# q and k parts as eight products with one store each, and attention's first loads and tiles moved into the last batch of the first layer

## What is computed

```python
# layer 0: a feed-forward block whose weights are picked per batch by an index
h = gelu(x @ Wi[e] + bi[e]);  o = h @ Wo[e] + bo[e]         # 256 -> 1024 -> 256
x = layernorm(o + x) * g[e] + be[e]
# layer 1: a transformer block
x = layernorm(x) * (1 + scale) + shift                      # from a time-step embedding
q, k, v = heads(x @ Wq + bq), heads(x @ Wk + bk), heads(x @ Wv + bv)   # 16 heads of 16
scores = q / 4 @ k.T + attention_bias                       # bias: 8 x 16 x 512 x 512 f32, 134 MB
scores = where(src_mask, -inf, scores)
x = x + (softmax(scores) @ v) @ Wo + bo
x = x + gelu2((layernorm(x) * g2 + beta2) @ W1 + b1) @ W2 + b2
```

## Time and profile before

| | us |
|---|---|
| median of 3 runs (lowest, highest) | 1185.88 (1183.18, 1190.21) |
| the profiled execution, its own time | 1181.05 |
| its span in the trace | 1179.2 |
| mean granted clock of PE | 0.957 |

### The profile page before, as it was taken

The page is one execution under the profiler, slowest core; times in us unless marked ns, Lnnn a source line. Parts: engine busy times, 40 slices in busy tenths (PEclk is TensorE's granted clock), DMA queues, the critical chain, the costliest instruction groups (busy, mean ns, idle before and its releaser), DMA issues.

```text
span 1179.2 us, 19133 instructions
## 1 busy us (share of the span) xinstructions
PE 1046.2 (89%) x6884; PEld 769.3 (65%) x6916; DVE 910.2 (77%) x2017; ACT 770.6 (65%) x1253; POOL 657.0 (56%) x327
## 2 busy tenths in 40 slices
PE   5999999983486888989989989899899979999998
PEld 4878888882354545555545545455455659999998
DVE  5699999993877779888989888798888866555553
ACT  6765666641475777878878868688788834444433
POOL 2666766651656367787787766866767522222220
PEclk9999999995798899999999999899899989999999
DMA  7745777548388799899997889879878331221001
GB/s 249 242 147 175 237 247 243 179 158 295 117 294 289 274 315 292 283 316 293 303 277 270 290 277 300 279 241 333 291 247 295 108 125 55 57 69 37 19 19 36
DMA packets 87281, 252.65 MB, mean 214 GB/s; under 512 B 8194, under 2 KB 56066, under 8 KB 67602
## 3 DMA queue, kind: packets, MB, share of 16 engines
q1 hardware_dynamic: 87186, 251.43, 64.4%
HBM read 209.19 MB, written 42.22 MB: 213 GB/s over the span
## 4 chain that ended last, share of the span: by engine, by line
PE 51%; ACT 11%; DVE 10%; DMA 9%; issue 8%; SPq 7%; POOL 3%; DVEq 0%; ACTq 0%; POOLq 0%
PE psV L644 10%; PE psH L519 10%; PE psT L631 10%; PE psO L519 8%; SPq L252 7%; PE psS L621 6%; ACT t_bt L872 5%; DMA t_mk<-in_mask_Bx1xSxS_bk 4%; ACT t_pt L758 3%; PE psQ L519 2%; DMA t_bt<-in_fside_Bx16xSxS 2%; POOL t_bt L1405 2%; PE psA L519 2%; DVE psS L1190 2%; DMA t_ks<-sc_qk 1%
## 5 line engine op out<-in xcount | busy, mean ns | idle before, releaser
L1405 POOL TENSOR_TENSOR t_bt<-t_bt,t_mb 128x1024 f32<-128x1024 f32 x192 | 410.7, 2164 | 206.0 <-DMA t_bt<-in_fside_Bx16xSxS 205.7
L1190 DVE CUSTOM_DVE_ANT_0 psS<-psS,t_bt 128x512 f32<-128x512 f32 x512 | 347.9, 704 | 84.9 <-PE psS L621 61.6
L872 ACT ACTIVATE t_bt<-psS,t_nm 128x512 f32<-128x512 f32 x512 | 339.1, 698 | 58.2 <-DVE t_nm L1190 56.5
L631 PE MATMUL psT<-t_idf,t_bt 128*128 128x128 f32 x2048 | 318.3, 279 | 16.7 <-DVE t_pt L1200 14.7
L631 PEld LDWEIGHTS psT<-t_idf,t_bt 128*128 128x128 f32 x2048 | 261.7, 144 | 83.3 <-DVE t_pt L1200 26.9
L758 ACT ACTIVATE t_pt<-psT 128x512 f32<-128x512 f32 x307 | 185.2, 604 | 83.7 <-PE psT L631 81.1
L621 PE MATMUL psS<-t_ks,t_qs 96*128 96x512 bf16 x512 | 201.8, 394 | 24.2 <-ACT t_bt L872 15.2
L644 PE MATMUL psV<-t_pt,t_vs 128*17 128x512 f32 x1024 | 140.3, 623 | 32.5 <-ACT t_pt L758 26.8
L621 PEld LDWEIGHTS psS<-t_ks,t_qs 96*128 96x128 bf16 x512 | 50.2, 98 | 154.1 <-ACT t_bt L872 108.6
L1200 DVE COPY t_pt<-psT 128x512 f32<-128x512 f32 x205 | 140.6, 686 | 1.6 <-PE psT L631 1.3
L1336 POOL TENSOR_SCALAR t_crs<-t_cmv 128x4 f32<-128x4 f32 x8 | 4.2, 521 | 145.5 <-DVE t_cmv L987 145.5
(11 more groups left out here) (173 smaller groups left out, 2042.8 us busy)
## 6 DMA issues: line engine op xcount, KB each, us to landing
t_bt<-in_fside_Bx16xSxS SPq DMA_DIRECT2D x128, 1024.0 KB, 6.8
sc_qk<-t_parts SPq DMA_DIRECT2D x192, 128.0 KB
t_qs<-sc_qk SPq DMA_DIRECT2D x16, 768.0 KB, 10.7
t_ks<-sc_qk SPq DMA_DIRECT2D x16, 768.0 KB, 14.1
t_wo_f<-in_L_cond_Wo SPq DMA_DIRECT2D x8, 1024.0 KB, 9.4
t_wi_f<-in_L_cond_Wi SPq DMA_DIRECT2D x7, 1024.0 KB, 8.8
sc_v<-t_v SPq DMA_DIRECT2D x8, 544.0 KB, 5.0
t_vs<-sc_v SPq DMA_DIRECT2D x8, 544.0 KB, 8.5
```

Source lines behind the costliest of these rows:

```text
L631: ins = e.transpose(psT[n % NTB][:, kk, :], bt[u % NB][:, t, kk * 128:(kk + 1) * 128], idf[:, :])
L872: e.activation(p, psS[bank(n)][:, :], ACT.Exp, bias=nm[:, n % 16:n % 16 + 1], scale=-1.0).then_inc(a_exp, 1)
L1190: e.tensor_tensor_reduce(s, s, bt[u % NB][:, t, :], -1.0, 3.0e38, ALU.add, ALU.min, nm[:, n % 16:n % 16 + 1]).then_inc(v_max, 1)
L1405: e.tensor_tensor(bt[u % NB][:, hs, :], bt[u % NB][:, hs, :], mb[b % 2][:, hs, :], ALU.add).then_inc(g_M, 1)
```

## The change

- `TERMS` has two more pairs, (1, 2) and (2, 1): 8 products, K = 128 rows instead of 96, for each score matmul, each q and k load (1024 KB instead of 768 KB) and each batch's stores (32 x 128 KB of data instead of 24).
- A store of a term now takes both halves of the heads at once: 8 issues of 256 KB for q and 8 for k, instead of 12 and 12 of 128 KB. `PT`, the count that the waits compare with, follows (128 for 8 stores).
- In SBUF, the first two bias tiles, `qs0`, `ks0`, the mask and v now lie over `wi_f`, `wo_f`, `wi`, `xt` and `xT` alone, which are free before the last `down`.
- SP issues their loads in the last round of the first stage's loop (i = 7), before the stores of batch 5, waiting for the last use of each region. Bias tiles 2, 3 and 4 still wait for the last matmul.
- Three tiles of attention (`FIRST_TILES`) come before `turn_x2(6)` on PE, ACT and DVE, the mask is read on ACT before that too, and `MIX` is changed so that 18 tiles are done after its 15 steps as before.
- POOL adds the masks of units 0 and 1 before both roots of the last layernorms. The transposes of tiles wait for `v_r1` themselves.

```diff
-PT = 16 * 6 * NK
+PT = 16 * 8
-TERMS = [(0, 0), (0, 1), (1, 0), (1, 1), (0, 2), (2, 0)]
+TERMS = [(0, 0), (0, 1), (1, 0), (1, 1), (0, 2), (2, 0), (1, 2), (2, 1)]
-MIX = [0, 0, 1, 2, 1, 1, 2, 2, 1, 1, 1, 1, 1, 1, 1]
+FIRST_TILES = 3
+MIX = [0, 1, 1, 1, 1, 1, 2, 2, 1, 1, 1, 1, 1, 1, 0]
...
             def store_parts(b, n):
                 P.wait_ge(g_p2, 2 * b + n + 1)
                 for i, c in enumerate(TERMS):
-                    for k in range(NK):
-                        hs = slice(k * H // NK, (k + 1) * H // NK)
-                        load(d_p[n], sc_qk[b, n, i, :, hs, :].rearrange("d h s -> h d s"), parts[n][:, c[n], k, :])
+                    load(d_p[n], sc_qk[b, n, i].rearrange("d (k h) s -> h d k s", k=NK), parts[n][:, c[n], :, :])
...
+            def first_attention_loads():
+                P.wait_ge(g_wil, B + 1)
+                load_bias(0)
+                P.wait_ge(g_wol, B + 1)
+                load_bias(1)
+                P.wait_ge(p_hid, NM * B)
+                load_mask(0)
+                load_qk(0)
+                load_v(0)
...
+                if i == B - 1:
+                    first_attention_loads()
                 if i >= 2:
                     store_parts(i - 2, 0)
...
             P.wait_ge(p_down, NT * B)
-            load_mask(0)
-            load_bias(0)
-            load_qk(0)
-            for u in range(1, NB):
+            for u in range(2, NB):
                 load_bias(u)
-            load_v(0)
...
             first_stage()
-            turn_x2(B - 2)
             for t in range(NT):
                 read_mask0(t)
-            tail, at = first_stage_end(), 0
+            at = 0
+            while at < FIRST_TILES:
+                attention(at)
+                at += 1
+            turn_x2(B - 2)
+            tail = first_stage_end()
...
             first_stage()
-            nextm, at = 1, 0
+            nextm, at = 2, 0
+            add_mask(0)
+            add_mask(1)
             root(rs[0], mv[0], 1e-12, (v_var1, B), g_rs1)
-            add_mask(0)
             root(rs[1], mv[1], 1e-5, (v_var2, B), g_rs2)
```

More of the change, by code:

```diff
@@ L161, in program @@
             wi_s = [sbuf(st, f"wi{n}", [128, NK, I], F32R) for n in "hl"]
+            xt = sbuf(st, "xt", [128, NK, S])
+            xT = [sbuf(st, f"xT{n}", [128, NK, S], F32R) for n in "hl"]
             wo_s = [sbuf(st, f"wo{n}", [128, NM, D], F32R) for n in "hl"]
             hT = [sbuf(st, f"hT{n}", [128, NM, S], F32R) for n in "hl"]
-            xt = sbuf(st, "xt", [128, NK, S])
-            xT = [sbuf(st, f"xT{n}", [128, NK, S], F32R) for n in "hl"]
             xs = [sbuf(st, f"x{i}", [128, NT, D]) for i in range(2)]
@@ L194, in program @@
             psC = psV.rearrange("p (t g d) -> p t g d", t=NT, g=4)
-            bt = [sbuf(st, f"bt{i}", [128, NT, S]) for i in range(NB)]
+            bt = [sbuf(st, f"bt{i}", [128, NT, S]) for i in range(2)]
             qs, ks = [sbuf(st, "qs0", [KR, 8, S], BF16)], [sbuf(st, "ks0", [KR, 8, S], BF16)]
@@ L198, in program @@
             vs = [sbuf(st, "vs0", [128, NT, H, VW])]
+            bt += [sbuf(st, f"bt{i}", [128, NT, S]) for i in range(2, NB)]
             nm = sbuf(st, "nm", [128, 16])
@@ L359, in sync_program @@
             load(d_ssb, ss[:, :, :], sc_ss.unsqueeze(0).broadcast_to([128, B, 2 * D]))
-            for i in range(1, B):
-                next_wo(i + 1)
-                next_x(i + 2)
-                next_bi(i + 2)
-                next_small(i + 1)
-                next_xt(i + 2)
-                next_wi(i + 2)
-                if i >= 2:
-                    store_parts(i - 2, 0)
-                    store_parts(i - 2, 1)
-                    store_v(i - 2)
-                store_x2(i - 1)
             def load_bias(u):
@@ L397, in load_v @@
                 load(d_vb[b % 2], vs[b % 2][:, :, :, :].rearrange("p t h v -> p t (h v)"), sc_v[b])
+            def first_attention_loads():
[7 more added lines that the diff above has]
+                load_v(0)
+            for i in range(1, B):
+                next_wo(i + 1)
+                next_x(i + 2)
+                next_bi(i + 2)
+                next_small(i + 1)
+                next_xt(i + 2)
+                next_wi(i + 2)
+                if i == B - 1:
+                    first_attention_loads()
+                if i >= 2:
+                    store_parts(i - 2, 0)
+                    store_parts(i - 2, 1)
+                    store_v(i - 2)
+                store_x2(i - 1)
             def first_stage_over():
@@ L624, in turn_p @@
                 u, t = divmod(n, NT)
+                P.wait_ge(v_r1, B)
                 P.wait_ge(a_exp, n + 1)
@@ L709, in tensor_program @@
             first_stage()
+            P.wait_ge(v_hTl, 8 * B)
+            at = 0
+            while at < FIRST_TILES:
+                attention(at)
+                at += 1
             turn_x2(B - 2)
-            P.wait_ge(v_hTl, 8 * B)
-            P.wait_ge(v_r1, B)
-            tail, at = first_stage_end(), 0
+            tail = first_stage_end()
             for k in MIX:
@@ L1279, in vector_program @@
             side = norms(B - 1)
-            advance(side, 6)
+            advance(side, 1)
+            at = 0
+            while at < FIRST_TILES:
+                attention(at)
+                at += 1
             turn_x2(B - 2)
-            tail, at = first_stage_end(), 0
+            advance(side, 5)
+            tail = first_stage_end()
             for k in MIX:
```

1 line of the change is left out of this document (added).

## The result

| | before | after |
|---|---|---|
| median of all runs, us (lowest, highest) | 1180.67 (1172.0, 1190.21) | 1191.72 (1184.8, 1196.55) |
| profiled execution, own time | 1181.05 | 1194.09 |
| its span | 1179.2 | 1192.3 |
| mean granted clock of PE | 0.957 | 0.948 |
| busy us: PE, DVE, ACT, POOL | 1046.2, 910.2, 770.6, 657.0 | 1052.2, 886.5, 771.1, 658.3 |

Each median is of 20 executions, and the three of before that are shown further up are among its 20. The ratio is 1.0095, with a 95% interval of 1.0073 to 1.0117: the change costs about 11 us, and the 0.5% up to which the prediction called two times equal lies outside the interval. The median of before came out 5 us lower than that of the three, and almost at its profiled execution.

The account below looks back on a forecast made before the run. PE has half the chain, DMA and SP's queue 16%, with a hole of some 20 us behind the first stage. Terms 3 + 2 + 4 + 6 = +15 gave 1196 us, with the median's 4.8 us 1201; range 1168 to 1214.

Parts of the forecast that it names:

- The pace of a set: Stores over 8 heads use half of the 16 DMA engines, so the new set takes 25.1 us instead of 19.3.
- The first rival: Stores do not stay at half the engines; a set takes 15.1 us, giving a median of 1169; chance 0.17.
- the signs for being right: Profile after: half share with stores alone, 25 us sets, first score matmul near 271 to 275, batch 6's k behind stores.
- the signs for being wrong: Profile after: share near 1 during stores, sets under 20 us, or a first stage ending later than 268.
- the third rival: Everything at its upper bound, the longer set setting the first stage's period (+8): +31 in all, 1217 us; chance 0.13.
- 1. 128 rows: Score matmuls: 128 rows instead of 96 take about the same time, 0 us.
- 2. First stage: Longer stores delay DVE's subtraction by 0.8 us for each of batches 1 to 4: +3 us, bounds 0 and 8.
- 3. Junction: Between first stage and attention: k lands 20 us earlier, but longer sets and reordered loads use that up: +2 us.
- the third item of the list: Junction: batch 5's stores land at 296, so k's part 0 of batch 6 starts there instead of 297.18.
- 4. Stores of batch 7: At tile 44, the longer set delays bias tiles DVE already waits for: +4 us, between 0 and 5.8.
- 5. q and k loads: Attention: 0.52 MB more for each pair of loads delays bias tiles and DVE: +6 us.
- 6. The first tiles, `MIX`, POOL's masks: Junction: three tiles ahead, the new `MIX` and POOL's two masks ahead of the roots leave the work the same, 0 us.

Follow-up runs that it names:

- e4: Changed kernel with q and k rows reordered so that each store walks 128 rows on its outermost dimension instead of 8 heads: 1150.97 us, ratio 0.9732.
- e9: Changed kernel with the next batch's mask loaded four tiles earlier, at tile 24 of each 64 instead of 28: 1163.25 us, ratio 0.9832.
- e13: Changed kernel with seven products instead of eight, (2, 1) taken off the list: 1174.11 us, ratio 0.9956.
- e2: Kernel before with eight products and one store each, without the early loads and first tiles: 1208.99 us, ratio 1.0231.
- e1: Changed kernel with six products again, one store each, early loads and first tiles kept: 1159.2 us, ratio 0.9811.
- e3: Changed kernel that stores eight products but loads and multiplies only the first six: 1196.07 us, ratio 1.0119.
- e8: Kernel before with the next batch's mask loaded four tiles earlier, at tile 24 of each 64 instead of 28: 1158.38 us, ratio 0.9807.
- e6: e4 with six products instead of eight: 1151.41 us, ratio 0.9724 to the kernel before.
- e14: e7 with six products instead of eight: 1126.97 us, ratio 0.9571 to the kernel before.
- e7: e4 with the next batch's mask loaded four tiles earlier, at tile 24 of each 64 instead of 28: 1120.31 us, ratio 0.9478 to the kernel before.

## Why the prediction was right, and where not

The forecast was 1201 us, +15 in the profiled execution; it came to 1191.72, and +13.0. The time is in the range, and the direction was the one given 62%. About 5 us of the 9 by which the median missed are the base: I added 4.8 us for the median of three, and with 20 executions before has 1180.67. That the change itself came out so near is luck: two terms of the sum miss by more than ten us each, with opposite signs.

**The pace of a set** (half the engines, 25.1 us) holds where nothing else is under way. In the last batch, where no weights are loaded beside it, the set begun at 242.07 has landed at 267.1, 25.0 us; the share stays at 54%; e4 shows that the eight heads on the outermost dimension are the cause. The first rival is out, and its price was off too. e4 builds it, with sets of about 15 us (the last store of batch 1 is issued at 141.8, and these stores land after 2.2 to 4.9 us), and has a median of 1150.97, 18 us under the 1169 that I gave. Of the signs for being right, the first score matmul came late, at 281.94 instead of 271 to 275; the half share, k's part 0 of batch 6 behind the stores (305.17), unit 5's mask (347.84) and DVE's longer wait near tile 60 came. Of the signs for being wrong, the one for the third rival came: the first stage ends at 273.6, later than 268.

**1. 128 rows, 0:** right. PE's time grew by 6 us in all at a lower mean clock, a score matmul of 128 rows takes 397 ns on average against 394 with 96, and e9 is no slower in attention than e8.

**2. First stage, +3 (bounds 0 and 8):** the term that was mis-sized, it is 13.6 us. I took the set's 25.1 us from the earlier trace rows, sets at the end of the first stage and in the junction, and set them against the spare time of one batch. In the first stage Wi and the next x are still under way when a set begins, and v, the normed x and the next Wo come in before it has landed. The set of batch 1 takes 29.1 us where that of batch 4 takes 25.0: its issues take 22.09 us instead of 19.69, and the last one lands after 8.07 instead of 6.59. Then the loop of 29.1 + 7.7 us is longer than PE's 32.45, and each of three batches pays for it, by 4.4, 4.8 and 2.8 us. I had also taken DVE as what the next batch waits for; it is the chain over POOL's part 2 to SP's next issue. It is the mechanism of the third rival, at a higher price than the 8 us I gave it. e13 shows the threshold, e2 that the early loads have no part in it.

**3. Junction, +2 (bounds -4 and +6):** -10.2 us between batch 4's stores and unit 12. "19 of the 20 us are gone" was wrong. By unit 12 the early loads and tiles gave 366.3 - 387.8 = -21.5 us with six products (e1 against before) and 391.2 - 409.4 = -18.2 with eight (after against e2), and the longer sets cost 9.5 to 11.7 there. The step that failed is the third item of the list, the comparison of k's part 0 of batch 6 at 296 with the 297.18 of before, as if both were waits for stores. Before it was no such wait. Batch 5's set also took 30.2 us from its issue, not the 34.7 of my line-up: k landed 39.8 us behind the first store of batch 4 where I had 42.5, and the set landed 23.2 us behind k where I had 25.1. And POOL's masks delayed batch 6's stores less, 11.7 us behind k's part 0, where I had 13.5 and before it was 16.2. What followed was right: the set of batch 6 moved unit 5's tile on POOL by 5.5 us more (347.84 against 338.85, after 316.88 against 313.42).

**4. Stores of batch 7, +4 (0 to 5.8):** 5.7 us, at its upper bound (7.4 in the two profiles alone). From unit 12 to unit 16 the four kernels with eight narrow products (after, e2, e3, e9) need 28.3 to 30.1 us, the three with six (before, e1, e8) 22.7 to 24.2, and the means of the two groups differ by 5.7; seven products (e13) need 26.1. "No reserve there" was the right reading.

**5. q and k loads, +6:** nothing, or a gain. The volume grew but the time to land fell, from 10.7 and 14.1 to 9.2 and 11.2 us. I took the rates of bias loads, which have 128 rows, for q and k loads of 96 rows too, and never measured one of those. e3, e6 and e14 agree.

**6. The first tiles, `MIX`, POOL's masks, 0:** not shown. No run tried them apart from the early loads, so what I call the gain of the early loads is that of all of them together. The `MIX` of before sums to 16 tiles, not to the 18 that I gave above; with the three first tiles the changed kernel does 18 in the junction, two more than before. And a part of the junction's gain goes over POOL's masks, as the rows with e1 show.

So +3 +2 +4 +6 was in truth +13.6 -10.2 +5.7 +0, with +3.9 left over in profiles whose executions differ by several us. The reading that stood the test is the one about engines of the DMA; the one that failed was taking a duration from one stage into another.

## What to carry to other kernels

Look at the share as well as the rate of a stretch with a single kind of transfer: a share that stood at a half was engines that weren't used here, and putting 128 rows instead of 8 on a store's outermost dimension took the changed kernel from 1.0095 to 0.9732 here, more than either half of the change did. A transfer's duration holds for the stage in which it was read; before using it in a loop, add what else is in line there, and compare the whole loop (landing to next issue included) with the engine that paces it. And waits of 2 to 3 us that made TensorE stand still gave back about twice their length when they went, so look for such waits once a batch even where the busy shares are near 90%.

## What was not expected of the hardware

- A load of 96 rows of 8 KB moved 212 to 215 GB/s, one of 128 rows 418 to 429 GB/s, both at a share above 90%. The Trainium skill ("DMA: Bandwidth & Descriptors", "Why a DMA increments its semaphore by 16 and not by 1") has a tile of 96 partitions on 16 engines, as one of 128; the share agrees with that, but the rate halves all the same. Fewer bytes can take longer.
- A set of narrow stores leaves half of the DMA time unused (5 tenths in 38 of 40 slices of [138 to 158 us]), and yet wide transfers that are issued while its last stores are under way bring the share to 9 tenths (from 157 us on, some 2 us after the first of them is issued). What comes behind such a set in SP's order waits for its issues, of 1.3 us each for 256 KB, where SP needed 0.7 us for the same bytes over 128 rows (e4).
- The granted clock fell to 0.50, the level of 1.2 GHz, around one stop of PE of 4.5 us in attention, and was at 1.00 again by 547, less than 7 us after PE went on at 540.51. With the mask loaded earlier the mean over the span rose from 0.966 (e4) to 0.983 (e7).
